# One graph network kernel on one core: the order of its first stage, and a second bank for the projection behind its heads

## The chip, the core and the metric

The kernel runs on one core of one Trainium2 chip. The metric is the device time of one execution in microseconds (us), lower is better. It is taken as the median of several runs.

## The reference

Four graph layers over 2708 nodes with 512 features, each followed by a residual sum and a layer norm: `x = layernorm(x + layer(x, adj))`, in float32. Only the first layer and the entry to the second matter here:

- Layer 0, for each of 8 heads of 64 columns: `feats = x @ kernels[h]`, `a_s = feats @ attn_self[h]`, `a_n = feats @ attn_neigh[h]`, weights `exp(-(a_s[i] - a_n[j])**2) * (adj[i, j] > 0)`, divided by their row sums, times `feats`, plus a bias; then relu over all heads.
- Layer 1: `adj @ (x @ W) + b`.
- Layers 2 and 3 are attention layers over the same adjacency. Layer 2 scores nodes with `(x @ W[:512]) @ a_w` and `(x @ W[512:]) @ a_w`, layer 3 with products of its own W with the vectors V. These products of weights and vectors depend on no data, so they can be formed at any time before they are used.

## The kernel before, in words

Nodes are padded to 2816, 22 tiles of 128 (`T`). The program is a row of blocks; each block has an instruction stream per engine, written out by hand with semaphores, and ends with all engines meeting. Loops over tiles are unrolled: `pair_loop` runs eleven pairs, buffer q = tile mod 2.

**First stage** (lines 196 to 334). SyncE (SP) loads the layer's weights `w0x`, two vectors, the identity, and then for each tile j the x tile (line 226, once tile j-2 has been transposed) and the transposed adjacency rows `al` (line 228, 1408 KB, once the mask of tile j-2 is done). GpSimd sends at the start for three vectors and three weight pieces that layers 2 and 3 will need (lines 233 to 239). TensorE transposes tile j into the bank `etp` (line 138), then multiplies tile j-1 with `w0x` into the two banks `pj` and `sc` (`project`, line 153), which waits until VectorE has emptied both banks of the tile before (`proj_out`). ScalarE copies each transposed tile to `xt` (line 144). VectorE first does six folds: a fold multiplies weights by a vector (line 292) and sums over a head (line 296). The first two folds add 8 columns for each half of `w0x`, and tile 0's product waits for them (`fold_sum`, line 255). The other four make `u2` and `u3` for layers 2 and 3; they wait for GpSimd's seven loads (line 307). Then for each tile j it turns the adjacency into a byte mask (line 329) and copies the banks of tile j-1 out (`feats_out`, lines 317 to 322). The buffers of the folds lie in `HB`, which is free until the heads write to it.

**The heads** (lines 338 to 522) follow, and are not touched.

**The projection behind the heads** (lines 551 to 621). For each tile j VectorE adds the bias (576), does relu and the residual sum (579), `bn_stats` (170), `bn_aggr` (173), adds epsilon (175), waits for GpSimd's power (184), normalises into `xn` (179), and then takes the low part of tile j-1: the product minus its rounded high part (587). GpSimd does the power and stores the normalised tile (541). TensorE waits for the normalised tile, transposes it (138), waits for ScalarE's copy (144) and multiplies with `w_sb` into the one bank `pj` (153). ScalarE copies the transposed tile, then rounds the product into `HR`, the high part (620). TensorE may write the bank again only when VectorE's low part of the tile before is done. SP loads the x tiles again (566).

**The stage after it** (from line 624) begins with loads of its weights and of the adjacency tiles.

Of the kernel before, what the change touches and what calls it, by code (L numbers as in the profile page):

```python
# [13 lines left out]
FP32 = mybir.dt.float32  # L14
F32R = mybir.dt.float32r
U8 = mybir.dt.uint8
ALU = mybir.AluOpType
# [3 lines left out]
N = 2708  # L21
# [55 lines left out]
def build(nc, x, adj_rows, adj_cols, adj_tiles, ident, w0, a0_self, a0_neigh, b0, w1, b1, w2a, w2b, a2_w, a2_b,  # L77
# [31 lines left out]
    with top:  # L109
# [57 lines left out]
        def ln_tile(dve, n, q, R, st, xn):  # L167

            dve.wait_ge(r_full, n + 1)
            dve.bn_stats(st[q][:, 0:6], R[q][:, :]).then_inc(ln_stats, 1)  # L170
            carry(dve, set_const, 1)
            dve.wait_ge(ln_stats, n + 1)
            dve.bn_aggr(st[q][:, 6:8], st[q][:, 0:6]).then_inc(ln_mean, 1)
            dve.wait_ge(ln_mean, n + 1)
            dve.tensor_scalar(st[q][:, 8:9], st[q][:, 7:8], LN_EPS, None, ALU.add).then_inc(ln_var, 1)
            dve.wait_ge(ln_rstd, n + 1)
# [19 lines left out]
        with ExitStack() as ph:  # L196
# [16 lines left out]
            with nc.Block() as block:  # L213
                @block.sync
                def _(sp):
# [6 lines left out]
                    def body(i):  # L222
                        for q in (0, 1):
                            j = 2 * i + q
                            wait(sp, turned, j - 1)
                            sp.dma_start(xin[q][:, :], x[j]).then_inc(x_in[q], 16)
                            wait(sp, mask_done, j - 1)
                            sp.dma_start(al[q][:, :], adj_cols[j]).then_inc(adj_in[q], 16)
# [3 lines left out]
                def _(pool):  # L232
                    pool.dma_start(vecs[2], a2_w.partition_broadcast(128)).then_inc(u_in, 16)
# [39 lines left out]
                def _(act):  # L273
                    def body(i):
                        for q in (0, 1):
                            keep_turned(act, 2 * i + q, xt[q])
                    pair_loop(act, body, first=2)
# [4 lines left out]
                def _(dve):  # L282
# [19 lines left out]

                    dve.wait_ge(w_in, 32)
                    dve.wait_ge(vec_in, 48)
                    fold(lambda k: w0x[:, k, :, 0:D // 2], vecs[1], F0, w0x[:, :, 0, D // 2:D // 2 + H0], KT)
                    fold(lambda k: w0x[:, k, :, 0:D // 2], vecs[0], F0, w0x[:, :, 1, D // 2:D // 2 + H0], KT)
                    dve.wait_ge(u_in, 7 * 16)
                    fold(lambda k: halves(wld[:, k, :]), vecs[2], D, u2[:, :, 0:1], KT)
                    fold(lambda k: halves(wld[:, 4 + k, :]), vecs[2], D, u2[:, :, 1:2], KT)
                    fold(lambda k: halves(wld[:, 8, :]), vecs[3], D3, u3[:, :, 0].unsqueeze(1), 1)  # L310
                    fold(lambda k: halves(wld[:, 8, :]), vecs[4], D3, u3[:, :, 1].unsqueeze(1), 1)
# [13 lines left out]
                    def body(i):  # L325
                        for q in (0, 1):
                            j = 2 * i + q
                            dve.wait_ge(adj_in[q], 16 * (i + 1))
                            dve.tensor_scalar(msk[:, j, :], al[q][:, :], 0.0, FAR, ALU.is_le, ALU.mult)\
                               .then_inc(mask_done, 1)  # L330
                            if not (isinstance(i, int) and j == 0):
                                feats_out(j - 1)
                    pair_loop(dve, body, first=True)
# [209 lines left out]
        def normed(dve, n, i, q, R, st, xn, phase):  # L543
            ln_tile(dve, n, q, R, st, xn)
            wait(dve, xn_stored[q], 16 * (phase * PAIRS + i))
            wait(dve, turned, n + T - 1)
            ln_write(dve, n, q, R, st, xn[q][:, :])

# [3 lines left out]
        with ExitStack() as ph:  # L554
            R, xn, st, xin, xt, bias, w_sb = norm_buffers(ph)
            c_in = sem("e0_in")
            with nc.Block() as block:
# [12 lines left out]
                def _(dve):  # L570
                    dve.wait_ge(c_in, 32)

                    def body(i):
                        for q in (0, 1):
                            j = 2 * i + q
                            dve.tensor_tensor(R[q][:, :], HB[0:P, j, :], bias[:, :], ALU.add).then_inc(r_half, 1)
                            dve.wait_ge(r_half, j + 1)
                            dve.wait_ge(x_in[q], 16 * (PAIRS + i + 1))
                            dve.scalar_tensor_tensor(out=R[q][:, :], in0=R[q][:, :], scalar=0.0, in1=xin[q][:, :],
                                                     op0=ALU.max, op1=ALU.add).then_inc(r_full, 1)  # L580
                            normed(dve, j, i, q, R, st, xn, 0)
                            if not (isinstance(i, int) and j == 0):
                                h_out(j - 1)

                    def h_out(j):
                        dve.wait_ge(h_hi, j + 1)
                        dve.tensor_tensor(HL[:, j, :], pj[0:P, :], HR[:, j, :].bitcast(FP32), ALU.subtract)\
                           .then_inc(proj_out, 1)
                    pair_loop(dve, body, first=True)
                    h_out(T - 1)  # L590
# [11 lines left out]
                def _(pe):  # L602
                    pe.wait_ge(c_in, 32)

                    def body(i):
                        for q in (0, 1):
                            j = 2 * i + q
                            pe.wait_ge(ln_done, j + 1)
                            turn_tile(pe, T + j, xn[q])
                            project(pe, T + j, xt[q], w_sb, (D,))  # L610
                    pair_loop(pe, body)

                @block.scalar
                def _(act):
                    def body(i):
                        for q in (0, 1):
                            j = 2 * i + q
                            keep_turned(act, T + j, xt[q])
                            act.wait_ge(proj_mm, T + j + 1)
# [1250 lines left out]
```

## Time and profile before

| | us |
|---|---|
| three runs | 3454.18, 3456.7, 3467.5 |
| their median | 3456.7 |
| the profiled execution's own time | 3455.23 |
| its span in the trace | 3453.4 |
| first stage, first load to last copy | 0.7 to 150.3 |
| projection behind the heads, first addition to last low part | 988.5 to 1110.2 |

| engine | busy us | share of the span |
|---|---|---|
| TensorE matmul | 3077.8 | 89% |
| TensorE weight load | 2184.4 | 63% |
| VectorE | 2604.7 | 75% |
| ScalarE | 1953.4 | 57% |
| GpSimd | 255.4 | 7% |

The span is the profiled execution from its first to its last instruction; the time of the runs is a little longer. The shares are averages over stages with different limits. Matmuls are pipelined and the ends of their records are modelled, so records can overlap. PE is TensorE's matmul, PEld its weight load, DVE VectorE, ACT ScalarE, POOL GpSimd, SP SyncE; SPq and POOLq are DMAs sent for from there.

### The profile page before, as it was taken

Reading aid. Unit: us, or ns where it says so; the run is one execution under the profiler, and the core shown is the slowest. Engines: PE = TensorE matmul, PEld = TensorE weight load, DVE = VectorE, ACT = ScalarE, POOL = GpSimd, SP = SyncE. Lnnn points to the kernel's source line nnn. Section 1 sums busy time; section 2 is a strip of 40 time slices with the busy share of each in tenths; the row PEclk is TensorE's granted clock in tenths of the full one; section 3 lists DMA queues with packets and bytes.
Section 4 is the critical chain, followed back from the end, with each engine's and each line's share of the span. In section 5 each row is a group of like instructions: output and inputs, shape, how many; then the busy total and the mean of one; then the engine's idle time right before and its main releaser. Section 6 shows DMA issues by size and latency. Waiting matters only on the chain. (4 is left out here: it accounts for less than half of the span.)

```text
span 3453.4 us, 38132 instructions
## 1 busy us (share of the span) xinstructions
PE 3077.8 (89%) x14683; PEld 2184.4 (63%) x14683; DVE 2604.7 (75%) x3257; ACT 1953.4 (57%) x1740; POOL 255.4 (7%) x441
## 2 busy tenths in 40 slices
PE   5799999999977999994999986999999966999994
PEld 4533333333333777773888865888888725898993
DVE  5599999999955566665777746888888655788877
ACT  0299999999932221112444427888888414566652
POOL 0000000000011111111000010000101000000003
PEclk9999999999999999997999997999999988999997
DMA  7600000000023576667333328676767522888884
GB/s 274 235 15 11 17 9 16 16 16 8 8 73 119 203 267 256 246 245 272 136 128 107 127 70 319 240 278 242 279 245 271 206 89 75 297 295 290 290 286 156
DMA packets 143059, 581.08 MB, mean 168 GB/s; under 512 B 16016, under 2 KB 30067, under 8 KB 124704
## 3 DMA queue, kind: packets, MB, share of 16 engines
q1 hardware_dynamic: 120288, 443.45, 35.7%
q0 software_dynamic: 22592, 135.19, 10.9%
q8 instruction: 119, 1.95, 0.2%
q14 instruction: 60, 0.49, 0.0%
HBM read 374.87 MB, written 203.71 MB: 168 GB/s over the span
## 5 line engine op out<-in xcount | busy, mean ns | idle before, releaser
L516 PE MATMUL bank<-dist,hf 128*65 128x512 f32 (+2 forms) x2112 | 805.1, 543 | 12.3 <-ACT dist L478 12.3
L516 PEld LDWEIGHTS bank<-dist,hf 128*65 128x65 f32 x2112 | 290.5, 138 | 518.9 <-issue 484.0
L1387 PE MATMUL bank<-pt,HA 128*128 128x256 f32 x1936 | 505.7, 381 | 4.5 <-DMA HA<-features 4.5
L478 ACT ACTIVATE dist<-dist 128x1408 f32<-128x1408 f32 (+1 forms) x352 | 452.9, 1322 | 4.6
L1656 DVE TENSOR_TENSOR w<-w,whi 128x1280 fp32r<-128x1280 f32 (+1 forms) x176 | 282.6, 1619 | 93.0 <-ACT whi L1616 92.2
L1314 DVE COPY pt<-bank 128x512 f32<-128x512 f32 (+1 forms) x440 | 264.3, 630 | 113.3 <-PE bank L1375 111.5
L1387 PEld LDWEIGHTS bank<-pt,HA 128*128 128x128 f32 x1936 | 328.9, 191 | 28.2 <-DMA HA<-features 4.7
L1616 ACT ACTIVATE whi<-w 128x1280 fp32r<-128x1280 f32 (+1 forms) x176 | 242.8, 1380 | 181.0 <-DMA w<-weights 178.8
L409 DVE TENSOR_TENSOR dist<-msk,sB 128x1408 f32<-128x1408 uint8 (+1 forms) x208 | 324.8, 1562 | 23.4 <-PE bank L516 13.9
L1375 PE MATMUL bank<-idt,v 128*128 128x128 f32 x1936 | 302.0, 276 | 41.6 <-ACT v L1261 33.6
L469 ACT ACTIVATE dist<-dist,neg_t 128x1408 f32<-128x1408 f32 (+1 forms) x208 | 295.1, 1419 | 60.1 <-DVE dist L409 56.8
L1582 PE MATMUL bank<-whi,EH 128*128 128x256 f32 x968 | 285.5, 295 | 40.4 <-DVE w L1656 38.4
L1375 PEld LDWEIGHTS bank<-idt,v 128*128 128x128 f32 x1936 | 242.9, 142 | 106.8 <-issue 31.3
L1306 DVE CUSTOM_DVE_ANT_0 v<-v,rows 128x2708 f32<-128x2708 f32 x88 | 268.2, 3048 | 18.7 <-DMA rows<-rows_low 11.9
L1583 PE MATMUL bank<-w,EH 128*128 128x256 f32 x968 | 275.5, 285 | 0.0
L1584 PE MATMUL bank<-whi,EL 128*128 128x256 f32 x968 | 275.5, 285 | 0.0
L144 ACT ACTIVATE xt<-bank 128x512 f32<-128x512 f32 x88 | 52.6, 598 | 371.4 <-PE bank L138 370.3
L1256 ACT ACTIVATE v<-fB,f 128x2708 f32<-128x2708 f32 x88 | 222.2, 2550 | 69.6 <-PE bank L1375 59.0
L412 DVE SCALAR_TENSOR_TENSOR dist<-msk,neg_t,sB 128x1408 f32<-128x1408 uint8 (+1 forms) x144 | 250.1, 1737 | 0.8 <-PE bank L516 0.4
L1261 ACT ACTIVATE v<-v,nm 128x2708 f32<-128x2708 f32 x88 | 224.0, 2547 | 15.7 <-POOL nm L1239 15.4
L1582 PEld LDWEIGHTS bank<-whi,EH 128*128 128x128 f32 x968 | 186.8, 193 | 47.4 <-issue 32.2
L686 PE MATMUL bank<-HR,hi 128*128 128x512 f32 x484 | 200.0, 413 | 17.7 <-ACT hi L793 17.7
(168 smaller groups left out, 5104.8 us busy)
## 6 DMA issues: line engine op xcount, KB each, us to landing
weights<-pt SPq DMA_DIRECT2D x220, 512.0 KB, 3.8
w<-weights SPq DMA_DIRECT2D x88, 768.0 KB, 6.9
w<-weights SPq DMA_DIRECT2D x88, 640.0 KB, 5.5
al<-in_adj_cols SPq DMA_DIRECT2D x22, 1408.0 KB, 8.3
at<-in_adj_tiles SPq DMA_DIRECT2D x22, 1408.0 KB, 7.9
rows<-in_adj_rows SPq DMA_DIRECT2D x22, 1408.0 KB, 6.8
HB<-in_adj_rows POOLq DMA_DIRECT2D x22, 1354.0 KB, 7.6
rows_low<-HB POOLq DMA_DIRECT2D x22, 1354.0 KB, 5.9
```

The lines of the kernel that those rows point to most:

```text
L409: dve.tensor_tensor(d[:, 0:VALID[c]], msk[:, m, c * CW:c * CW + VALID[c]], sB[hh][:, 0:VALID[c]], ALU.add).then_inc(d_ready, 1)
L469: act.activation(d[:, 0:VALID[c]], d[:, 0:VALID[c]], ACT.Square, bias=neg_t[0:P, m, bass.ds(hp * 2 + hh, 1)]).then_inc(sq_act, 1)
L478: act.activation(d[:, 0:VALID[c]], d[:, 0:VALID[c]], ACT.Exp, scale=-1.0).then_inc(p_ready, 1)
L516: mm = pe.matmul(sums_bank(hh, k)[0:FW, 0:hi - a * P], hf[hh][:, m, :], d[:, a * P:hi], start=(m == 0), stop=(m == T - 1))
L1306: dve.tensor_tensor_reduce(s[:, 0:N], s[:, 0:N], rows[r][:, :], 1.0, LOW, ALU.mult, ALU.max, mx[:, u % 16:u % 16 + 1]).then_inc(mx_ready, 1)
L1314: dve.tensor_copy(dst, src).then_inc(kept_dve, 1)
L1375: t = pe.transpose(ring[index % len(ring)][:, (m - a) * P:(m - a + 1) * P], slot(u)[:, m * P:(m + 1) * P], idt[:, :])
L1387: t = pe.matmul(acc_t[n % 2][:, 0:P2], HA[:, m, h * D3:(h + 1) * D3], pt[n % 2][:, m, :, :].rearrange("p r n -> p (r n)"), start=(m == 0), ...
L1582: pe.matmul(into, EH[:, m, h * D3:(h + 1) * D3], hi, start=(m == 0), stop=False)
L1583: pe.matmul(into, EH[:, m, h * D3:(h + 1) * D3], lo, start=False, stop=False)
L1584: t = pe.matmul(into, EL[:, m, h * D3:(h + 1) * D3], hi, start=False, stop=(m == T - 1))
L1656: dve.tensor_tensor(w[k % WS][:, 0:b - a, :], w[k % WS][:, 0:b - a, :].bitcast(FP32), whi[k % HS][:, 0:b - a, :].bitcast(FP32), ALU.subtra ...
```

## The change

In the first stage:

- SP no longer loads x tiles from tile 2 on; ScalarE sends for x tile j+2 right after its copy of tile j. SP loads 2708 columns of adjacency per row instead of 2816, and the mask covers these alone.
- GpSimd's seven loads wait until two masks are done.
- The masks of tiles 0 and 1 are made behind the first and the second fold. The four later folds are done one each behind the copies that VectorE makes in the turns of tiles 10, 12, 14 and 16.

In the projection behind the heads:

- The banks `pj` and `sc` take the products in turn.
- TensorE transposes tile j+1 before it multiplies tile j. ScalarE makes the high part of tile j-1 behind its copy of tile j.
- VectorE takes the low part of tile j-3 in the turn of tile j, between adding epsilon and the wait for the power; the last three low parts follow the loop.

```diff
 # ln_tile is split: ln_moments is its first part, up to the wait for ln_rstd
+        def ln_moments(dve, n, q, R, st):
...
+        def ln_tile(dve, n, q, R, st, xn):
+            ln_moments(dve, n, q, R, st)
             dve.wait_ge(ln_rstd, n + 1)
 # first stage, SyncE
-                            wait(sp, turned, j - 1)
-                            sp.dma_start(xin[q][:, :], x[j]).then_inc(x_in[q], 16)
+                            if j < 2:
+                                sp.dma_start(xin[q][:, :], x[j]).then_inc(x_in[q], 16)
                             wait(sp, mask_done, j - 1)
-                            sp.dma_start(al[q][:, :], adj_cols[j]).then_inc(adj_in[q], 16)
+                            sp.dma_start(al[q][:, 0:N], adj_cols[j][:, 0:N]).then_inc(adj_in[q], 16)
 # first stage, GpSimd
+                    pool.wait_ge(mask_done, 2)
                     pool.dma_start(vecs[2], a2_w.partition_broadcast(128)).then_inc(u_in, 16)
...
 # first stage, ScalarE
                             keep_turned(act, 2 * i + q, xt[q])
+                            if 2 * i + q + 2 < T:
+                                act.dma_start(xin[q][:, :], x[2 * i + q + 2]).then_inc(x_in[q], 16)
 # first stage, VectorE
+                    def mask(j):
+                        dve.wait_ge(adj_in[j % 2], 16 * (j // 2 + 1))
+                        dve.tensor_scalar(msk[:, j, 0:N], al[j % 2][:, 0:N], 0.0, FAR, ALU.is_le, ALU.mult).then_inc(mask_done, 1)
+
+                    def fold_later(k):
+                        if k == 0:
+                            dve.wait_ge(u_in, 7 * 16)
+                        if k < 2:
+                            fold(lambda c: halves(wld[:, 4 * k + c, :]), vecs[2], D, u2[:, :, k:k + 1], KT)
+                        else:
+                            fold(lambda c: halves(wld[:, 8, :]), vecs[1 + k], D3, u3[:, :, k - 2].unsqueeze(1), 1)
...
                     fold(lambda k: w0x[:, k, :, 0:D // 2], vecs[1], F0, w0x[:, :, 0, D // 2:D // 2 + H0], KT)
+                    mask(0)
                     fold(lambda k: w0x[:, k, :, 0:D // 2], vecs[0], F0, w0x[:, :, 1, D // 2:D // 2 + H0], KT)
-                    dve.wait_ge(u_in, 7 * 16)
...
+                    mask(1)
...
-                            dve.wait_ge(adj_in[q], 16 * (i + 1))
-                            dve.tensor_scalar(msk[:, j, :], al[q][:, :], 0.0, FAR, ALU.is_le, ALU.mult)\
-                               .then_inc(mask_done, 1)
-                            if not (isinstance(i, int) and j == 0):
+                            if j >= 2:
+                                mask(j)
+                            if j > 0:
                                 feats_out(j - 1)
+                            if 10 <= j < 18 and j % 2 == 0:
+                                fold_later(j // 2 - 5)
 # projection behind the heads
+            into = (pj, sc)
 # VectorE
+                    for j in range(T):
...
+                        ln_moments(dve, j, q, R, st)
+                        if j >= 3:
+                            h_out(j - 3)
+                        dve.wait_ge(ln_rstd, j + 1)
+                        wait(dve, xn_stored[q], 16 * (j // 2))
+                        wait(dve, turned, T + j - 1)
+                        ln_write(dve, j, q, R, st, xn[q][:, :])
+                    for j in range(T - 3, T):
+                        h_out(j)
 # TensorE
+                    turn_next(0)
+                    for j in range(T):
+                        if j + 1 < T:
+                            turn_next(j + 1)
+                        pe.wait_ge(turned_out, T + j + 1)
+                        wait(pe, proj_out, T + j - 1)
+                        for k in range(KT):
+                            t = pe.matmul(into[j % 2][0:P, :], xt[j % 2][:, k, :], w_sb[:, k, :],
+                                          start=(k == 0), stop=(k == KT - 1))
+                        t.then_inc(proj_mm, 1)
 # ScalarE
+                    for j in range(T):
+                        keep_turned(act, T + j, xt[j % 2])
+                        if j > 0:
+                            high(j - 1)
+                    high(T - 1)
```

## Rows read from the trace of the kernel before

**Rows 1.** Windows: stretch, length, busy us (instructions) by engine, PEclk, DMA share, GB/s.

```profile
18.00:24.00 6.00, 1.09 (x4) 0.72 (x4) 5.01 (x6) 0.60 (x1) 0.00 (x0) 1.00 1.03 422
60.00:130.00 70.00, 60.69 (x289) 49.44 (x288) 36.10 (x72) 8.36 (x14) 0.00 (x0) 1.00 0.93 341
990.00:1110.00 120.00, 97.62 (x264) 42.07 (x264) 76.67 (x152) 26.16 (x44) 25.20 (x44) 0.96 0.28 92
```

**Rows 2.** Timeline, a steady tile of the first stage: start us, duration, engine, line.

```profile
52.43 3.80 PE L153 MATMUL bank<-w0x,xt 128*128 128x264 f32 x16 [0.65 <-ACT xt L144]
...
56.06 0.60 PE L138 MATMUL bank<-idt,xin 128*128 128x128 f32 x4
56.27 0.42 DVE L317 COPY HA<-bank 128x256 f32<-128x256 f32 x1 [1.72 <-PE bank L153]
...
56.75 0.41 DVE L322 COPY HA<-bank 128x256 f32<-128x256 f32 x1
...
57.31 3.80 PE L153 MATMUL bank<-w0x,xt 128*128 128x264 f32 x16 [0.65 <-ACT xt L144]
59.11 1.63 DVE L329 TENSOR_SCALAR msk<-al 128x2816 uint8<-128x2816 f32 x1 [1.95 <-DMA al<-in_adj_cols]
```

**Rows 3.** Waits of the first stage, 46 to 145 us: total, times, longest.

```profile
DVE msk L329 <- DMA al<-in_adj_cols: 40.7, 20, 3.7
```

**Rows 4.** Timeline, a steady tile of the projection behind the heads.

```profile
1006.63 0.68 DVE L576 TENSOR_TENSOR R<-HB,bias 128x512 f32<-128x512 f32 x1
...
1006.86 3.67 PE L153 MATMUL bank<-w_sb,xt 128*128 128x512 f32 x8 [0.86 <-DVE HL L587]
...
1009.08 0.15 DVE L175 TENSOR_SCALAR st<-st 128x1 f32<-128x1 f32 x1
...
1009.93 0.55 DVE L179 TENSOR_SCALAR xn<-R,st 128x512 f32<-128x512 f32 x1 [0.69 <-POOL st L184]
...
1010.53 0.66 PE L138 MATMUL bank<-idt,xn 128*128 128x128 f32 x4
1010.57 0.60 ACT L620 ACTIVATE HR<-bank 128x512 fp32r<-128x512 f32 x1 [3.93 <-PE bank L153]
...
1011.20 0.69 DVE L587 TENSOR_TENSOR HL<-bank,HR 128x512 fp32r<-128x512 f32 x1 [0.73 <-ACT HR L620]
...
1011.81 0.68 DVE L576 TENSOR_TENSOR R<-HB,bias 128x512 f32<-128x512 f32 x1
```

**Rows 5.** Timeline, start of the first stage.

```profile
18.92 2.50 DVE L292 TENSOR_TENSOR HB<-w0x,HB 128x512 f32<-128x512 f32 x4 [17.72 <-DMA idt<-in_ident]
...
21.46 2.29 DVE L296 TENSOR_REDUCE w0x<-HB 128x32 f32<-128x2048 f32 x1
...
28.65 5.87 PE L153 MATMUL bank<-w0x,xt 128*128 128x264 f32 x16 [3.15 <-DVE w0x L296]
...
41.17 3.15 DVE L329 TENSOR_SCALAR msk<-al 128x2816 uint8<-128x2816 f32 x2
...
45.28 6.07 PE L153 MATMUL bank<-w0x,xt 128*128 128x264 f32 x16 [10.33 <-DVE HA L322]
```

**Rows 6.** Timeline, last copy of the first stage.

```profile
149.88 0.41 DVE L322 COPY HA<-bank 128x256 f32<-128x256 f32 x1
```

**Rows 7.** DMA issues, first 12 us: count, KB each, median us to landing.

```profile
al<-in_adj_cols SPq DMA_DIRECT2D x2, 1408.0 KB, 19.6
...
idt<-in_ident SPq DMA_DIRECT2D x1, 64.0 KB, 15.1
```

**Rows 8.** DMA issues in the projection behind the heads.

```profile
x_after<-xn POOLq DMA_DIRECT2D x19, 256.0 KB, 2.3
xin<-in_x SPq DMA_DIRECT2D x16, 256.0 KB, 2.6
```

**Rows 9.** Timeline, first product and last low part of the projection.

```profile
994.25 5.93 PE L153 MATMUL bank<-w_sb,xt 128*128 128x512 f32 x8 [0.69 <-ACT xt L144]
...
1109.53 0.69 DVE L587 TENSOR_TENSOR HL<-bank,HR 128x512 fp32r<-128x512 f32 x1 [4.48 <-ACT HR L620]
```

More of the change, by code:

```diff
@@ L165, in keep_rows @@
             act.activation(rows_sb[0:width, :], etp[0:width, 0:128], ACT.Copy).then_inc(rows_out, 1)
-        def ln_tile(dve, n, q, R, st, xn):
+        def ln_moments(dve, n, q, R, st):
             dve.wait_ge(r_full, n + 1)
@@ L305, in _ @@
                     fold(lambda k: w0x[:, k, :, 0:D // 2], vecs[1], F0, w0x[:, :, 0, D // 2:D // 2 + H0], KT)
+                    mask(0)
                     fold(lambda k: w0x[:, k, :, 0:D // 2], vecs[0], F0, w0x[:, :, 1, D // 2:D // 2 + H0], KT)
-                    dve.wait_ge(u_in, 7 * 16)
[L308 to L311, printed above, removed]
+                    mask(1)
                     dve.wait_ge(set_const, 1 + H0)
@@ L541, in norm_store @@
             pool.dma_start(dst[2 * i + q], xn[q][:, :]).then_inc(xn_stored[q], 16)
[L543 to L547, printed above, removed]
         L1 = ExitStack()
@@ L571, in _ @@
                     dve.wait_ge(c_in, 32)
[L573 to L583, printed above, removed]
                     def h_out(j):
                         dve.wait_ge(h_hi, j + 1)
-                        dve.tensor_tensor(HL[:, j, :], pj[0:P, :], HR[:, j, :].bitcast(FP32), ALU.subtract)\
+                        dve.tensor_tensor(HL[:, j, :], into[j % 2][0:P, :], HR[:, j, :].bitcast(FP32), ALU.subtract)\
                            .then_inc(proj_out, 1)
-                    pair_loop(dve, body, first=True)
-                    h_out(T - 1)
+                    for j in range(T):
+                        q = j % 2
+                        dve.tensor_tensor(R[q][:, :], HB[0:P, j, :], bias[:, :], ALU.add).then_inc(r_half, 1)
+                        dve.wait_ge(r_half, j + 1)
+                        dve.wait_ge(x_in[q], 16 * (PAIRS + j // 2 + 1))
+                        dve.scalar_tensor_tensor(out=R[q][:, :], in0=R[q][:, :], scalar=0.0, in1=xin[q][:, :],
+                                                 op0=ALU.max, op1=ALU.add).then_inc(r_full, 1)
+                        ln_moments(dve, j, q, R, st)
[7 more added lines that the diff above has]
+                        h_out(j)
                 @block.gpsimd
@@ L603, in _, with turn_next, high @@
                     pe.wait_ge(c_in, 32)
[L605 to L611, printed above, removed]
+                    def turn_next(j):
+                        pe.wait_ge(ln_done, j + 1)
+                        turn_tile(pe, T + j, xn[j % 2])
+                    turn_next(0)
[8 more added lines that the diff above has]
+                        t.then_inc(proj_mm, 1)
                 @block.scalar
                 def _(act):
[L615 to L619, printed above, removed]
-                            act.activation(HR[:, j, :], pj[0:P, :], ACT.Copy).then_inc(h_hi, 1)
-                    pair_loop(act, body)
+                    def high(j):
+                        act.wait_ge(proj_mm, T + j + 1)
+                        act.activation(HR[:, j, :], into[j % 2][0:P, :], ACT.Copy).then_inc(h_hi, 1)
+                    for j in range(T):
[3 more added lines that the diff above has]
+                    high(T - 1)
         with ExitStack() as ph:
```

## The prediction

> **What bounds the kernel now.** I read the page first. The chain that ended last covers only the last 57 us, so it says nothing of the two stages that the change touches; they have to be read by themselves, from the timeline, and summed, because every stage ends in a barrier and what one stage saves reaches the end. I found the stages by the starts of their lines: the first stage runs from 0 to 150.3 us, the projection behind the heads from 988.5 to 1110.2 us. The windows [rows 1] show that neither fills an engine: TensorE's records sum to 0.81 of the second, at a mean granted clock of 0.96, and the DMA engines are 0.93 busy in the middle of the first, moving 341 GB/s.
>
> The steady tile of the **first stage** [rows 2] takes 4.88 us (52.43 to 57.31). TensorE multiplies for 3.80 us, then VectorE copies both banks out, 56.27 to 57.16, and only then TensorE goes on: its transposes and ScalarE's copy lie beside that. One pair of banks makes the two engines alternate. The change leaves that as it is. VectorE has 40.7 us of idle time before 20 masks [rows 3], 2.0 us each, waiting for the adjacency tile. This is slack: the mask at 59.11 ends at 60.74, before the product ends at 61.1. It is little slack, so the transfers are nearly a second bound.
>
> The steady tile of the **second stage** [rows 4] takes 5.18 us (1006.63 to 1011.81) and is a ring: product 3.67, ScalarE's high part 0.60, VectorE's low part 0.69, semaphores 0.2. VectorE stands idle 0.69 us for GpSimd's power and 0.73 us for the high part. TensorE idles while the one bank is emptied.
>
> **The change, part by part.**
>
> *Start of the first stage.* The first fold waits for the last vector load and starts at 18.92; the product of tile 0 starts at 28.65, when two folds are done; four more folds then hold VectorE until the masks at 41.17, and tile 1's product starts only at 45.28 [rows 5]. So tile 0 lies there finished for 10 us. The stage's last copy starts at 149.88 and ends at 150.29 [rows 6].
>
> The seven GpSimd loads (two matrices of 1.05 MB, one of 0.26, three vectors of 0.26: 3.15 MB) now start after the second mask. Until then the SP queue is alone. Before, SP's 5.05 MB and these 3.15 MB, 8.2 MB together, had landed by 6.9 + 19.6 = 26.5 us at the latest (the two first adjacency tiles: mean landing 19.6 after issues at 5.47 and 6.68, the later landing 21.0) [rows 7], from 2.5 us on: 342 GB/s. Without 3.15 MB, that is 9.2 us less, so the first adjacency tile is there at about 17.3; the 4% it loses (2708 columns for 2816) gives 0.3. The identity, the last thing the fold waits for, landed at 3.7 + 15.1 = 18.8; before it go 1.64 MB of SP. I take 10 us (bounds: 8, if nothing shares; 18.8, if nothing is gained). Fold of four products and a sum: 2.50 + 2.29 + 0.06 = 4.85. So fold 10 to 14.9, mask 0 from 17.0 to 18.6, second fold to 23.5, product of tile 0 at 23.6 instead of 28.65. Mask 0 has taken a place in front of the product: 1.6 us plus 2.1 us of waiting, which I charge.
>
> *Then no gap.* Product 0 at the low clock 5.87 as in [rows 5], copy and semaphores 1.2: tile 1 starts at 30.7. Its product took 6.07 at the low clock after a 10 us rest; now there is no rest, so I take 3.80 (if not, +2.3). From tile 1's start, 21 tiles of 4.88 are 102.5: 133.2.
>
> *The four later folds* now follow the copies at tiles 10, 12, 14 and 16. Natural distance from one copy's end to the next one's start is 3.95. With a fold of 4.85 and a mask of 1.6 between them it is 6.5, so the two large ones cost 2.55 each, 5.1 together; TensorE, waiting for its banks, is who waits. The two small ones are about a quarter as long (1.2 to 1.4) and fit into the 2.0 us in which VectorE now waits for a tile. Adjacency transfers get ahead meanwhile. The 3.15 MB behind the second mask fall on tiles 2 to 5; in front, tile 2's adjacency may be issued 20 us earlier than before. I charge 1 us for masks that come late there. End of the stage: 133.2 + 5.1 + 1 = 139.3, **gain 11.0**. Bounds: 15 (identity and tile at their earliest, no late masks) and -1 (loads no earlier: fold 18.9 to 23.8, mask 0 from 26.5 to 28.1, product 0 at 33.0; and tile 1 at the low clock: the end comes to 151).
>
> *x tiles from ScalarE.* 20 DMA issues leave SP and go behind ScalarE's copies. An issue takes 0.3 to 1.1 us; ScalarE idles 4.3 us per tile, so it costs nothing there. The tile is sent for 0.65 us later than from SP, needed 9.8 us after the transposes that free it, and landed in 8.0; its wait fell short only once by 0.3 us. SP no longer stands between two waits. I cost it at nothing; if landings grew by 2 us every tile would lose about 1, which is inside the bounds above.
>
> *Second stage.* Two banks break the ring, and the low part is taken three tiles back, inside VectorE's wait for the power. VectorE's tile: 1006.63 to 1009.93 is 3.30 with that wait in it; the wait from the start of the variance to the normalising is 0.85, and variance 0.15 + low part 0.69 + 0.05 is 0.89, so +0.04; normalising 0.55: 3.89 [rows 4]. TensorE's tile: product 3.67 less the 0.17 by which the next transposes overlap its end [rows 2], transposes 0.66 less the same 0.17 at their end: 3.99. Bounds: 3.76 (VectorE's tile without the low part and its 0.13 of joints) and 4.33 (TensorE's two rows added without overlap). I take 4.0, TensorE's side. ScalarE has 1.2 of work in it. Nothing else comes up: a store lands in 2.3 and an x tile in 2.6 [rows 8], against two periods less an operation, 7.
>
> TensorE now transposes tile 1 before product 0. Tile 1 is normalised at 996.14, so product 0 starts near 997.3 instead of 994.25 [rows 9] and, at the low clock, ends at 1003.3; low part 0 is then late by about 1 us on VectorE, once. Product 1 goes 1003.9 to 1007.5, product 2 starts at 1008.0. Nineteen periods of 4.0 on, product 21 starts at 1084.0, ends 1087.7, and high and low part add 1.4: 1089.1 against 1109.53 + 0.69 = 1110.2. **Gain 21.1**, bounds 14 (period 4.33, and 1 more lost at the start) and 26 (period 3.76).
>
> *The sum.* The profiled execution took 3455.2 us with a span of 3453.4, which is 1.5 below the median 3456.7 and inside the three runs. 3455.2 - 11.0 - 21.1 = 3423.1.
>
> **Rivals.**
>
> *Transfers bind the first stage.* From 18.6 on there are 20 adjacency tiles of 1.387 MB, 20 x tiles of 0.26 and the 3.15 MB: 36.1 MB. At 341 GB/s they take 106 us, to 124.5, and some 10 us of latency, mask, copies and last product follow: 134, which does not bind. Below 325 GB/s it does; at 300 the stage ends at 148 and the time is 3432. For it: only two adjacency tiles are ever in flight, and the mix now comes from three queues. Against: the engines moved 422 GB/s from 18 to 24 us [rows 1]. The Trainium skill's "DMA: Bandwidth & Descriptors" (Specifications) puts a core's share of HBM at about 358 GB/s; by it all 41.1 MB of the stage need an estimated 115 us whatever the order, ending near 127, so no binding either, but only 12 us below my figure. The window with 422 GB/s stands above that limit for 6 us. Chance 0.12.
>
> *The second stage keeps a hand-off.* If TensorE waits each tile for the normalising (a chain of variance, GpSimd, normalising, transposes), the period comes to about 4.6, midway between 4.0 and today's 5.18: 0.6 x 19 = 11 us less gain, 3434. For it: the two engines stand within 0.1 us of each other. Against: VectorE may run up to two tiles ahead. Chance 0.12.
>
> *Slower: TensorE's clock.* Product 0 shows 5.93 us at 1.2 GHz after a rest against 3.67 [rows 9, 4], transposes 1.09 against 0.6. If the new order, with transposes between waits, kept the clock down, a tile would take 7.0, 3.0 over the forecast: from 11 of the 22 tiles on the whole gain of 32 is gone, with all 22 it is 3423 + 66 = 3489. Against: with gaps of 0.85 each tile the granted clock after the start is 2.4 GHz, and gaps get shorter. Chance 0.02.
>
> *The change does less than it says.* The loads land no earlier, mask 0 delays the second fold, and product 0 starts at 33.0: the first stage then ends at 148.7 and the time is 3432. Chance 0.06.
>
> **How the numbers follow.** Forecast 0.68, at 3423. The range has 3414 below (4 to 5 us better in either stage) and 3436 above, which takes in both rivals at their middle. A measurement of this kernel can tell about 0.5%, 17 us, from no change. Faster by more than that needs half the gain: the forecast and nearly all of the first, second and fourth cases, 0.94. Within 0.5%: both stages at their lower bounds, or the clock low for some 6 to 16 tiles, 0.04. Slower: 0.02.
>
> **What the profile would show.** First fold near 10 us, product 0 near 23.6, no gap between tiles 0 and 1, two tiles of 7.4 us at 10 and 12, last copy near 139. Second stage: products every 4.0 us, no wait of VectorE's low part on ScalarE's high part, VectorE's idle time before the normalising gone, about 100 us from first addition to last low part. Wrong: a mask that waits over 2 us for its tile in mid stage; a product record of 5.9 past the first; a change of more than 3 us in any other stage.

## The result, and the profile after

The changed kernel took 3423.03 us (median of 4, 3416.31 to 3429.03), the kernel before 3455.44 on the same chip. The ratio is 0.9899, with a 95% interval of 0.9869 to 0.9929: 24 to 45 us less. The prediction was 3423 us, the range 3414 to 3436. The agreement to 0.1 us is luck, as the two stages show: together they gained 36 us and not 32.

These are points of the two traces, in us from the start. The stages end where their last copy or low part ends; the adjacency stage is taken from the first to the last weight load of its first group of products.

| | before | after | gained |
|---|---|---|---|
| end of the first stage | 150.29 | 139.56 | 10.7 |
| heads, to the projection's first addition | 838.2 | 837.1 | 1.1 |
| projection, first addition to last low part | 121.7 | 96.4 | 25.3 |
| from there to the adjacency products | 16.3 | 16.6 | -0.3 |
| adjacency products | 450.9 | 458.6 | -7.7 |
| rest | 1876.0 | 1872.9 | 3.1 |
| span | 3453.4 | 3421.2 | 32.2 |

The timeline of the first stage's start, changed kernel, answers to [rows 5]:

```profile
11.34 2.50 DVE L297 TENSOR_TENSOR HB<-w0x,HB 128x512 f32<-128x512 f32 x4 [10.14 <-DMA idt<-in_ident]
...
16.08 1.56 DVE L310 TENSOR_SCALAR msk<-al 128x2708 uint8<-128x2708 f32 x1
...
22.42 5.92 PE L153 MATMUL bank<-w0x,xt 128*128 128x264 f32 x16 [5.38 <-DVE w0x L301]
...
29.49 3.80 PE L153 MATMUL bank<-w0x,xt 128*128 128x264 f32 x16 [0.71 <-ACT xt L144]
...
34.37 3.80 PE L153 MATMUL bank<-w0x,xt 128*128 128x264 f32 x16 [0.65 <-ACT xt L144]
...
39.56 0.66 PE L138 MATMUL bank<-idt,xin 128*128 128x128 f32 x4 [1.39 <-DMA xin<-in_x]
...
40.06 3.73 PE L153 MATMUL bank<-w0x,xt 128*128 128x264 f32 x16
...
41.48 1.57 DVE L310 TENSOR_SCALAR msk<-al 128x2708 uint8<-128x2708 f32 x1 [2.37 <-DMA al<-in_adj_cols]
...
45.97 3.73 PE L153 MATMUL bank<-w0x,xt 128*128 128x264 f32 x16
```

The first fold starts at 11.34 for 18.92. Mask 0 follows at once: its tile had landed. The first product starts at 22.42 for 28.65, and the second at 29.49 for 45.28. Products 3 and 4 (40.06 and 45.97, each some 5.8 us after the one before) come late because the transposes in front of them wait for an x tile; the mask at 41.48 waits for its adjacency tile too. Beside those tiles the deferred loads are under way. Their landings, from the DMA issues of 13 to 60 us (count, KB each, median us to landing):

```profile
xin<-in_x ACTq DMA_DIRECT2D x9, 256.0 KB, 6.7
...
HB<-in_w2b POOLq DMA_DIRECT2D x1, 1024.0 KB, 15.9
...
HB<-in_w POOLq DMA_DIRECT2D x1, 256.0 KB, 18.6
```

The two long folds, same kernel and view, and the end of the stage, for [rows 6]:

```profile
74.96 2.48 DVE L297 TENSOR_TENSOR HB<-HB 128x512 f32<-128x512 f32 x4
...
77.48 2.29 DVE L301 TENSOR_REDUCE u<-HB 128x4 f32<-128x2048 f32 x1
...
82.20 3.80 PE L153 MATMUL bank<-w0x,xt 128*128 128x264 f32 x16 [2.77 <-DVE HA L336]
...
94.09 5.49 PE L153 MATMUL bank<-w0x,xt 128*128 128x264 f32 x16 [2.77 <-DVE HA L336]
...
139.15 0.41 DVE L336 COPY HA<-bank 128x256 f32<-128x256 f32 x1
```

Each fold of 4.8 us leaves TensorE waiting 2.77 us where it waits 0.65 otherwise: 2.13 us. After the second wait one product takes 5.49 us for 3.80. The granted clock of that stretch, below that of the product after the first wait (windows, columns as in [rows 1]):

```profile
82.00:86.00 4.00, 3.80 (x18) 3.27 (x19) 1.53 (x2) 0.00 (x0) 0.00 (x0) 1.00 0.93 348
94.10:99.40 5.30, 5.30 (x16) 4.15 (x17) 1.32 (x1) 0.00 (x0) 0.00 (x0) 0.68 0.99 372
```

Each stretch lies within one product and its transposes. At a mean of 0.68 of 2.4 GHz, part of the second one ran at 1.2 GHz. TensorE had just waited 2.77 us, but it had waited as long before the first one, which ran at full clock.

A steady tile of the projection behind the heads answers to [rows 4]:

```profile
1002.30 0.60 PE L138 MATMUL bank<-idt,xn 128*128 128x128 f32 x4
...
1002.50 0.60 ACT L635 ACTIVATE HR<-bank 128x512 fp32r<-128x512 f32 x1 [2.79 <-PE bank L627]
...
1002.74 3.60 PE L627 MATMUL bank<-w_sb,xt 128*128 128x512 f32 x8
1002.78 0.15 DVE L174 TENSOR_SCALAR st<-st 128x1 f32<-128x1 f32 x1
...
1003.13 0.69 DVE L583 TENSOR_TENSOR HL<-bank,HR 128x512 fp32r<-128x512 f32 x1 [0.19 <-ACT HR L635]
...
1003.74 0.54 DVE L181 TENSOR_SCALAR xn<-R,st 128x512 f32<-128x512 f32 x1
...
1004.19 0.69 DVE L588 TENSOR_TENSOR R<-HB,bias 128x512 f32<-128x512 f32 x1
...
1006.61 3.60 PE L627 MATMUL bank<-w_sb,xt 128*128 128x512 f32 x8
```

High part, low part and normalising now lie beside the product of another tile. Products start every 3.87 us for 5.18, with transposes right behind them and no idle time named: TensorE sets the period. VectorE waits 0.19 us for the high part of three tiles back and nothing for the power. The stage's first product and its end, for [rows 9]:

```profile
985.27 5.58 PE L627 MATMUL bank<-w_sb,xt 128*128 128x512 f32 x8
...
1072.40 0.69 DVE L583 TENSOR_TENSOR HL<-bank,HR 128x512 fp32r<-128x512 f32 x1 [2.74 <-ACT HR L635]
```

### The profile page after: what moved, and what is told of

The parts are those of the page before. It is cut to its first block and busy times, and to the rows that moved or that the text cites. A ratio compares the mean times of both kernels' runs of the same rounds, so it can differ in the third digit from the quotient of the medians.

```text
span 3421.2 us, 38132 instructions
## 1 busy us (share of the span) xinstructions
PE 3070.5 (90%) x14683; PEld 2188.8 (64%) x14683; DVE 2599.8 (76%) x3257; ACT 1951.7 (57%) x1740; POOL 257.2 (8%) x441
```

## The experiments

Twelve kernels were run. Each is told by its edit against the changed kernel, unless it says otherwise. The runs of one kernel spread over 6 to 22 us, so stages are read in the traces; this table has all of them in us ("slow products" counts products of 5 us or more in the first stage, without the first one). loads_at_start, low_two_back, low_behind_norm, x_from_sp, two_pairs and masks_behind were each run once, the others four to six times.

| kernel | first stage's last copy starts | projection | adjacency products | slow products |
|---|---|---|---|---|
| before | 149.9 | 121.7 | 450.9 | 1 (6.07, [rows 5]) |
| changed | 139.2 | 96.4 | 458.6 | 1 |
| first_only | 140.5 | 121.2 | 449.3 | 2 |
| second_only | 149.5 | 96.3 | 454.8 | 1 |
| loads_at_start | 147.4 | 96.4 | 449.9 | 2 |
| folds_in_pieces | 135.8 | 96.2 | 447.5 | 0 |
| low_two_back | 139.3 | 137.9 | 464.8 | 1 |
| low_behind_norm | 139.0 | 102.9 | 448.0 | 1 |
| x_from_sp | 140.5 | 97.0 | 456.0 | 1 |
| two_pairs | 128.9 | 96.4 | 447.5 | 1 |
| pieces_pairs | 127.9 | 96.5 | 451.1 | 2 |
| pp_spread | 127.9 | 96.6 | 441.8 | 1 |
| pp_three | 124.8 | 96.5 | 455.0 | 1 |
| masks_behind | 141.6 | 96.5 | 449.4 | 2 |

**Do the parts add?** `first_only` has the projection of before:

```diff
-            into = (pj, sc)
...
-                        if j >= 3:
-                            h_out(j - 3)
+                            normed(dve, j, i, q, R, st, xn, 0)
+                            if not (isinstance(i, int) and j == 0):
+                                h_out(j - 1)
```

> The first stage as changed, the projection behind the heads as before. Theory (the two parts are independent, each gains in its own stage): last copy of the first stage near 139.6 us, as in the changed kernel, the projection again 121.7 us from first addition to last low part with 5.18 us a tile, whole time 3455.4 - 10.7 = 3445, within the scatter of the runs. Rival (a saving in the first stage is given back in the heads or later): heads longer than 838 us, time near 3455.

3444.5 us, ratio 0.9956 (0.9941 to 0.9971): 15 us less. Last copy at 140.5, projection 121.2, heads 837.4. The theory holds; nothing is given back in the heads.

`second_only` has the first stage of before:

```diff
-                    pool.wait_ge(mask_done, 2)
...
-                            if 10 <= j < 18 and j % 2 == 0:
-                                fold_later(j // 2 - 5)
```

> The first stage as before, the projection with two banks and the low part three tiles back. Theory: projection 96.4 us for 121.7, 3.87 us a tile, first stage ends at 150.3, time 3455.4 - 25.3 = 3430. It also tells whether the stage that follows (adjacency times features), which took 458.6 us from its first to its last group in the changed kernel for 450.9 before, is longer because the projection is denser (then it is near 458 here and near 451 with the first part alone) or by chance of TensorE's granted clock (then any of the two).

3437.7 us, ratio 0.9933 (0.9914 to 0.9952): 23 us less. The projection takes 96.3. 15 and 23 make 38, the whole change 35 by its ratio: they add within their intervals. The adjacency stage took 454.8 here, 449.3 with the first part alone, and 441.8 to 464.8 over all kernels with the new projection, with no edit to it: its length scatters, and 450.9 and 449.3 with the old projection lie inside that scatter. Two stretches of it in the changed kernel (windows):

```profile
1209.00:1249.00 40.00, 40.00 (x179) 32.53 (x178) 25.85 (x42) 8.00 (x8) 6.51 (x12) 1.00 0.69 264
1369.00:1409.00 40.00, 33.53 (x139) 27.19 (x138) 22.58 (x39) 5.89 (x6) 5.45 (x10) 0.91 0.59 200
```

The same 40 us hold 139 matmuls at a mean clock of 0.91 and 179 at 1.00. The clock is not all of it: TensorE is also idle for 6.5 us in the second stretch. The changed kernel's timeline shows what it waits for:

```profile
1387.45 0.55 POOL L793 DMA_DIRECT2D HB<-in_adj_rows  x1 [10.08 <-DMA rows_low<-HB]
...
1389.70 0.55 DVE L181 TENSOR_SCALAR xn<-R,st 128x512 f32<-128x512 f32 x1 [8.40 <-POOL st L186]
...
1390.30 1.11 PE L138 MATMUL bank<-idt,xn 128*128 128x128 f32 x4 [6.47 <-DVE xn L181]
```

GpSimd stands 10.08 us until a store of its own, `rows_low`, has landed, and makes the power only after that; VectorE waits for the power, TensorE for the normalised tile, and the transposes behind the wait take 1.11 us, as at the low clock, for 0.60. That store took 10.3 us to land, where the median of the 21 in this stage is 5.8. Over the fourteen traces TensorE is idle for 15 to 32 us of the stage and at the low clock for 5 to 31 us. As an estimate, the idle time and half the low-clock time taken off the stage's length leave 418 to 424 us in every trace, for lengths of 442 to 465. pp_spread, the shortest, has no such landing over 8 us, and low_two_back, the longest, has four. So the 7.7 us lost there are the scatter of one execution, not a cost of the change. Why a store lands late now and then stays open.

**Were the early loads in the way?** `loads_at_start`:

```diff
-                    pool.wait_ge(mask_done, 2)
```

> The changed kernel, but GpSimd sends for its seven loads at the start. Theory (the loads hold up what the first product needs, the identity and then the first adjacency tile, since mask 0 now stands between the folds): first fold near 18.9 for 11.3, mask 0 near 26, first product near 32.5 for 22.4, then tiles 4 and 5 without the waits for x tiles (-1.8), last copy near 148. Rival (the early start comes from the smaller adjacency tiles and from the order on SyncE's queue): first product near 24, last copy near 140.

First fold at 19.3, first product at 30.4, last copy at 147.4. So taking the deferral away costs 8.2 us of the first stage's 10.7 (1.7 of them one slow product more here), and the theory holds, though mask 0 came at 24.0, not 26. Products 3 and 4 follow at 4.89 and 4.88 us: no x tile is late where the loads are not deferred.

**What do the long folds cost?** `folds_in_pieces` cuts the four later folds into eight pieces:

```diff
-                            if 10 <= j < 18 and j % 2 == 0:
-                                fold_later(j // 2 - 5)
+                            if 9 <= j < 17:
+                                fold_piece(*PIECES_0[j - 9])
```

A piece is three multiplications, or one and half of the sum, or half of the sum, or one of the two small folds.

> The changed kernel, but the four later folds are cut into eight pieces of at most 1.9 us, one behind each copy of tiles 8 to 15. Theory (a fold of 4.8 us makes TensorE wait 2.13 us for its banks, twice, and the clock falls after the second wait, +1.7 us on one product): no wait over 0.7 us at these tiles, last copy 4.3 us earlier from the waits, near 135.3, and 6.0 earlier, near 133.6, if the low clock at 94 us was due to them. Rival (the transfers become the bound when VectorE no longer gives them time): masks start to wait for adjacency tiles over 2 us and end the gain at 1 to 2 us.

3412.5 us, ratio 0.9870 (0.9852 to 0.9887). Last copy at 135.8: 3.3 us earlier, of the 6.0 named. No product waited for its banks at tiles 8 to 15 and none was slow. But both named outcomes came in part. The waits for x tiles at tiles 3 and 4 were 1.2 us longer than in the changed kernel, and products at tiles 13, 18 and 20 came some 1.5 us late in all, the first behind an x tile, the others behind copies. VectorE waited for adjacency tiles again, as the waits of 20 to 140 us show:

```profile
DVE msk L310 <- DMA al<-in_adj_cols: 16.2, 10, 3.1
```

In the changed kernel those waits are 4.6 us in 3 masks over the same 20 to 140 us, and 2.3 us from 46 to 145 us, for 40.7 in [rows 3]: the long folds had given the transfers time. The low clock: seven kernels have the two long folds with one pair of banks (changed, first_only, loads_at_start, x_from_sp, masks_behind, low_two_back, low_behind_norm). They hold 14 waits of TensorE of 1.8 to 2.8 us for a fold; nine of the products behind them were slow, and none of the products at those tiles here. So the low clock goes with the waits, though not with each. Waits for x tiles can be followed by it too (masks_behind below, and pieces_pairs, where a product of 5.41 follows a wait of 2.96 us).

**Is it the second bank or the distance?** `low_two_back`:

```diff
-                        if j >= 3:
-                            h_out(j - 3)
+                        if j >= 2:
+                            h_out(j - 2)
```

> The changed kernel with the low part taken two tiles back, not three, at the same place. Theory (the distance of three is what breaks the ring): normalising tile j-1, transposes 0.6, product 3.6, high part 0.6, low part 0.6, normalising tile j 0.5 close a ring of about 6.1 us a tile, slower than the 5.18 of one bank; projection near 140 us. Rival (the second bank alone gives the gain): 3.9 to 4.2 us a tile.

The ring closes, at 5.96 us a tile (high parts at 1020.37 and 1026.33), and the projection takes 137.9 us, 16 more than with one bank:

```profile
1020.37 0.60 ACT L635 ACTIVATE HR<-bank 128x512 fp32r<-128x512 f32 x1 [2.84 <-PE bank L627]
1021.00 0.69 DVE L583 TENSOR_TENSOR HL<-bank,HR 128x512 fp32r<-128x512 f32 x1 [2.29 <-ACT HR L635]
1021.60 0.54 DVE L181 TENSOR_SCALAR xn<-R,st 128x512 f32<-128x512 f32 x1
...
1022.20 0.66 PE L138 MATMUL bank<-idt,xn 128*128 128x128 f32 x4 [1.87 <-DVE xn L181]
...
1022.69 3.60 PE L627 MATMUL bank<-w_sb,xt 128*128 128x512 f32 x8
...
1026.33 0.60 ACT L635 ACTIVATE HR<-bank 128x512 fp32r<-128x512 f32 x1 [2.84 <-PE bank L627]
```

3479.4 us in one run, 18 slower than the kernel before beside it. The ring closes because TensorE transposes tile j+1 in front of product j, and so waits for a normalised tile that stands behind the low part of tile j-1. With this order, a second bank and the low part two tiles back cost time; three tiles back is what makes it pay. A second bank with the transposes in their old place was not run.

`low_behind_norm`:

```diff
-                        if j >= 3:
-                            h_out(j - 3)
                         dve.wait_ge(ln_rstd, j + 1)
...
                         ln_write(dve, j, q, R, st, xn[q][:, :])
+                        if j >= 3:
+                            h_out(j - 3)
```

> The changed kernel with the low part three tiles back, but behind the normalising of tile j and not in the wait for GpSimd's power. Theory: VectorE's tile grows by the 0.69 that no longer hides, 3.76 + 0.66 = 4.4 us, VectorE becomes the bound; projection near 96.4 + 19 x 0.55 = 107 us. Rival (TensorE's 3.87 is the bound with room to spare on VectorE): under 4.0 us a tile.

The period is 4.36 us as expected, with VectorE idle 0.69 us for the power again:

```profile
1021.63 0.55 DVE L181 TENSOR_SCALAR xn<-R,st 128x512 f32<-128x512 f32 x1 [0.69 <-POOL st L186]
1022.09 0.68 DVE L583 TENSOR_TENSOR HL<-bank,HR 128x512 fp32r<-128x512 f32 x1
...
1022.92 3.67 PE L627 MATMUL bank<-w_sb,xt 128*128 128x512 f32 x8
...
1025.99 0.55 DVE L181 TENSOR_SCALAR xn<-R,st 128x512 f32<-128x512 f32 x1 [0.69 <-POOL st L186]
```

But the stage took 102.9 us, not 107. The first seven products still came 3.87 us apart: VectorE was ahead when TensorE's first, slow product ended, and its lead was used up before its own period showed. So the place in the wait is worth 6.5 us here.

**Who should send for the x tiles?** `x_from_sp`:

```diff
-                            if j < 2:
-                                sp.dma_start(xin[q][:, :], x[j]).then_inc(x_in[q], 16)
+                            wait(sp, turned, j - 1)
+                            sp.dma_start(xin[q][:, :], x[j]).then_inc(x_in[q], 16)
...
-                            if 2 * i + q + 2 < T:
-                                act.dma_start(xin[q][:, :], x[2 * i + q + 2]).then_inc(x_in[q], 16)
```

> The changed kernel with the x tiles sent for by SyncE again, between the adjacency tiles. Theory (I costed the move to ScalarE at nothing): last copy of the first stage within 1 us of 139.6; the waits for x tiles at tiles 4 and 5 stay, since the deferred loads share the DMA engines with any queue. Rival (ScalarE's own queue gets the small tiles past the adjacency): x tiles land in over 8 us, transposes wait at several tiles, last copy 3 us or more later.

Last copy at 140.5, 1.3 us later, but not for the queue: product 10 starts at 75.11 for 75.19, and the 1.3 us are a slow product of 6.86 us behind the first long fold, where the changed kernel has one of 5.49 behind the second. The first product comes 0.9 us later (23.3), which is made up by tile 3. The x tiles landed in 6.0 us (median) for 5.8 from ScalarE. One wait for an x tile is left, of 0.4 us; product 4 comes 1.1 us late behind a copy. The theory's second half, that the waits stay, did not come out. So the queue matters little. The Trainium skill ("DMA: Bandwidth & Descriptors", Issuing engines are not separate DMA queues) says that the DMAs of all these engines run on the same 16 DMA engines and interleave, and the two medians agree.

**Is a first mask worth its place?** `masks_behind`:

```diff
                     fold(lambda k: w0x[:, k, :, 0:D // 2], vecs[1], F0, w0x[:, :, 0, D // 2:D // 2 + H0], KT)
-                    mask(0)
                     fold(lambda k: w0x[:, k, :, 0:D // 2], vecs[0], F0, w0x[:, :, 1, D // 2:D // 2 + H0], KT)
+                    mask(0)
                     mask(1)
```

> The changed kernel with the two first masks behind both folds, nothing else. Theory (mask 0 delays the second fold by its 1.6 us, and by its wait of none, since the adjacency tile landed first): first product at 20.9 for 22.4; the third adjacency tile is sent for 5 us later, at 22.7, so mask 2 at about 30 just meets its place; last copy 1 to 1.5 us earlier, near 138. Rival (the early mask is what keeps the transfers going): masks 2 to 4 wait for adjacency, last copy not earlier.

The first product came at 20.5, 1.9 us earlier, but the last copy at 141.6, 2.4 us later and not 1 to 1.5 earlier. Masks waited 11.0 us for adjacency from 20 to 140 us (4.6 in the changed kernel), transposes' weight loads 5.7 us in 4 for x tiles (3.9 in 2), and two products were slow (5.34 and 6.86, for one of 5.49). At product 5 the lead was down to 0.5 us. So the waits that the rival names are there: without the early mask the third adjacency tile is sent for at 21.97, with it at 17.67. But the slow products alone are 2.9 us more than in the changed kernel, which is all of the 2.4. Without them this one run would be 0.5 us ahead, so whether the early mask pays is open: the first of the slow products follows a wait of 2.13 us for an x tile and may belong to the order, the other stands behind a long fold, as in the changed kernel.

**What bounds the first stage next?** `two_pairs` lets its products take two pairs of banks in turn:

```diff
+            pair = ((pj, sc), (acc[0], acc[1]))
...
-                        project(pe, n, xt[q], w0x[:, :, :, :].rearrange("p k b c -> p k (b c)"),
-                                (D // 2 + H0, D // 2 + H0))
+                        pe.wait_ge(turned_out, n + 1)
+                        wait(pe, proj_out, n - 1)
```

> The changed kernel, and the first stage's products go to two pairs of banks in turn, so that VectorE's copies lie beside the next product. Theory (transfers are the next bound, close behind): TensorE could go on every 3.9 us, but a tile needs 1.65 MB, 4.8 us at the 341 GB/s seen before and 4.1 at 400; so 4.1 to 4.8 a tile with VectorE's masks waiting for adjacency again, last copy between 121 and 137. Rival (the transfers are not near their limit): 3.9 to 4.0 a tile, last copy near 119.

Last copy at 128.9, 3406.5 us in one run. Unhindered products are 4.0 us apart. The rest is waits of masks for adjacency, 33.9 us in 15, and of transposes for x tiles:

```profile
28.70 3.73 PE L266 MATMUL bank<-w0x,xt 128*128 128x264 f32 x16
32.26 0.60 PE L138 MATMUL bank<-idt,xin 128*128 128x128 f32 x4
32.70 3.73 PE L266 MATMUL bank<-w0x,xt 128*128 128x264 f32 x16
39.17 0.66 PE L138 MATMUL bank<-idt,xin 128*128 128x128 f32 x4 [2.75 <-DMA xin<-in_x]
39.66 3.73 PE L266 MATMUL bank<-w0x,xt 128*128 128x264 f32 x16
```

`pieces_pairs` is `two_pairs` with the pieces of `folds_in_pieces`:

> Folds in pieces and two pairs of banks in the first stage together. With two pairs alone the products came every 4.0 us, but at three places late: 4.9 us at tiles 3 and 4, which wait for x tiles beside the deferred loads, 2.9 us at two later waits, and 6 us of low clock near 110 us. Theory (transfers bound it): the pieces take away no transfer, so masks wait for adjacency as long as before, last copy 126 to 129 and time near 3404. Rival (the long folds cost there too, by late copies and the low clock after them): last copy near 121.

Last copy at 127.9: the theory's window. 3412.4 us, ratio 0.9854 (0.9829 to 0.9879). Masks wait for adjacency for 31.1 us (33.9 in two_pairs), so transfers bound it still, and the pieces that gave 3.3 us with one pair of banks give 1.0.

`pp_spread` is `pieces_pairs` with the deferred loads spread; this part is what it adds:

```diff
+                    pool.dma_start(ab2[:, :], a2_b.partition_broadcast(128)).then_inc(u_in, 16)
+                    pool.wait_ge(mask_done, 4)
                     pool.dma_start(wld[:, 0:4, :], w2a).then_inc(u_in, 16)
+                    pool.wait_ge(mask_done, 6)
                     pool.dma_start(wld[:, 4:8, :], w2b).then_inc(u_in, 16)
                     pool.dma_start(wld[:, 8, :], w3).then_inc(u_in, 16)
-                    pool.dma_start(ab2[:, :], a2_b.partition_broadcast(128)).then_inc(u_in, 16)
```

> The kernel pieces_pairs with the deferred loads spread: vectors after mask 1, the first matrix after mask 3, the second with the small one after mask 5. Theory (x tiles are late at tiles 3 and 4 because 3.15 MB stand beside them at once): the 4.9 us there fall to about 2, last copy 2 to 3 us earlier than in pieces_pairs. Rival (the transfers are near their limit all through, and it only matters that 3.15 MB are to be moved somewhere): waits appear at later tiles, last copy within 1 us.

The rival holds: products 3 and 4 come in time, product 5 is 3.8 us late and product 7 2.8, and the last copy is at 127.9 again. 3417.8 us, ratio 0.9871 (0.9848 to 0.9894).

`pp_three` is `pp_spread` with a third adjacency buffer; this part is what it adds:

```diff
-            al = [sb(ph, f"al{q}", [P, NP]) for q in (0, 1)]
+            al = [sb(ph, f"al{q}", [P, N]) for q in (0, 1, 2)]
...
-                            wait(sp, mask_done, j - 1)
+                            wait(sp, mask_done, j - 2)
```

> The kernel pp_spread with three adjacency buffers, so that three tiles can be in flight. Theory (bandwidth is the limit, 38 MB after the start at 341 to 390 GB/s need 98 to 111 us): nothing gained but jitter, last copy within 2 us. Rival (two tiles in flight bound the rate, by a landing of 8.3 us and a mask of 1.6 every two tiles, 4.95 us a tile): GB/s rises from about 331 to 380 and more, waits of masks for adjacency go, last copy 4 us or more earlier, near 118.

Last copy at 124.8, between the two. The waits of masks for adjacency are gone from the list (24.8 us in 13 in pp_spread, from 25 to 125 us), but the transposes' weight loads wait for x tiles 11.6 us in 8, for 9.6 in 4, and the x tiles land in 8.0 us (median) for 6.6. The windows of 65 to 115 us, when the deferred loads have landed, of pp_spread, then of pp_three, and of 25 to 50 us of pieces_pairs, with the deferred loads in them:

```profile
65.00:115.00 50.00, 47.51 (x234) 39.76 (x233) 36.65 (x70) 7.17 (x12) 0.00 (x0) 1.00 0.91 334
```

```profile
65.00:115.00 50.00, 45.89 (x225) 37.99 (x224) 38.91 (x72) 6.57 (x11) 0.00 (x0) 1.00 0.93 356
```

```profile
25.00:50.00 25.00, 22.04 (x98) 17.93 (x97) 10.60 (x24) 2.90 (x5) 2.37 (x5) 0.93 1.01 392
```

A third tile in flight raises 334 to 356 GB/s, so two in flight were part of the limit; the DMA engines stand at 0.93 busy, so little is left. With the deferred loads among them they moved 392 GB/s over 25 us. The Trainium skill ("DMA: Bandwidth & Descriptors", Specifications) has about 358 GB/s for a core's share of HBM; these 25 us are above it. 3410.1 us, ratio 0.9857 (0.9831 to 0.9882).

folds_in_pieces, pieces_pairs, pp_spread and pp_three are all below the changed kernel by their medians, by 5 to 13 us though run at another time, and beat the kernel before clearly. Their intervals overlap each other's and, narrowly, the changed kernel's, so which is fastest is open by whole times; by the trace of the first stage it is pp_three.

## Why the prediction was right

**Start of the first stage.** Right in kind, three sizes off. The fold starts at 11.34 and not 10: the identity landed 8.0 us after its issue at 3.2, so 1.64 MB of SyncE's loads need that by themselves. The first adjacency tile I had put at 17.0, and charged 2.1 us of waiting; it landed at 15.2 (issue at 4.18, 11.0 to landing), and mask 0 did not wait at 16.08. The starting point was wrong: in the kernel before, tile 0 landed at 23.7 (5.47 and 18.2) and tile 1 at 27.7 (6.68 and 21.0), so the 26.5 of the prediction is neither, and not "at the latest". The saving was nearly right: tile 0 came 8.5 us earlier for 9.5. The first product was so at 22.4 for 23.6.

**No gap.** Tile 1's product took 3.80, as taken, and the 10 us gap is gone.

**Late tiles.** I charged 1 us for late masks. Masks did wait, 2.37 and 2.02 us at 41.5 and 46.7, but the price was 1.8 us, and it came from x tiles: TensorE transposes tile j+1 ahead of tile j's product, so a late x tile holds a product that doesn't need it. I had weighed the x tiles' landings only in the middle of the stage.

**Long folds.** 2.13 us each for 2.55: fold and mask follow each other with less between them than I put. The low clock behind, 1.7 us here, was no term of the sum. Sum of the stage: 29.5 + 102.5 + 1.8 + 4.3 + 1.7 = 139.8 against 139.56 measured and 139.3 forecast.

**x tiles from ScalarE.** Costed at nothing, and x_from_sp agrees: up to product 10 it is 0.1 us ahead.

**Projection.** The mechanism was right and the term for the period too large: 3.87 for 4.0. By the tile shown, 3.60 for the product less 0.17 of overlap and 0.60 for the transposes less 0.16 make 3.87. The form of the sum was right; the records of before, 3.67 and 0.66, come from transposes and products that had waited and are each 0.06 to 0.07 longer. Over 19 periods the 0.13 is 2.5 us. Product 2 also started 18.3 us after the stage's first addition and not 19.5: product 0 came at 8.6 for 8.8 and was shorter, 5.58 for 6.0, and less lay between the next ones. The rest of the 4.2 us is in the tail. Balance: TensorE is the bound and VectorE has 0.2 to spare.

**Rivals.** Transfers did not bind the first stage as it was changed, but do once anything else is faster (two_pairs to pp_three). The hand-off on TensorE did not come. The clock did not stay low in the projection: only its first product is slow. It did show, as lost microseconds, in single products after waits.

**What I named as wrong.** All three signs appeared, in part. Masks waited over 2 us for their tiles twice, but early, beside the deferred loads; after 47 us the longest such wait is 0.24. A product past the first was slow, of 5.49 us and not 5.9, which cost 1.7 us. And a stage elsewhere changed by more than 3 us, the adjacency stage (the rest, 3.1, holds many stages). That one is scatter between executions, and it hid the 4 us that the projection gained beyond the forecast. The whole time was right because two errors of that size met.

## What to carry to other kernels

Here a second output bank broke the ring between TensorE and the engines that empty it only when the low part was taken so late that its own release was not waited for; write out the ring with the distance in tiles before choosing it, since one tile too near made it slower than a single bank. Loads that nobody needed yet cost their bytes in front of the first product, and wherever they were moved beside double-buffered tiles they cost waits; a place where the DMA engines are idle was not tried. Sum a change by stage from traces when whole times scatter by 10 to 20 us, and follow the longest waits of a stage that scatters to their first releaser.

## What was not expected of the hardware

- After waits of 1.8 to 2.8 us for a fold, nine of 14 products ran 5.5 to 6.9 us for 3.8, at a mean granted clock of 0.68 in the window shown, while in low_two_back waits of 1.9 us in every tile left the products at 3.60.
- An untouched stage of 450 us scattered from 442 to 465 us between executions. What differs is TensorE's idle time and low clock behind stores that GpSimd waits for: their median landing is 5.8 to 6.0 us, and up to four of the 21 in a trace take 8 to 11.
- The DMA engines moved 392 GB/s for 25 us with three queues in use, and on the adjacency and x tiles alone 334 with two adjacency tiles in flight and 356 with three, at shares of 0.91 and 0.93.
